# The combine stage's thirteen groups start with one node tile instead of ending with it

## The reference

```
x = x + ffn(layernorm(x))          # two experts per node, weighted
...
deg = count of each src;  dinv = (deg + 1) ** -0.5
msg = layernorm(x)[dst] * dinv[src] * dinv[dst]
agg = segment_sum(msg, src)        # self loops included
x = x + relu(agg @ W.T + b)
```

## Time and profile before

| what | value |
|---|---|
| runs, median (lowest to highest) | 1460.05 us (1455.34 to 1467.41) |
| the profiled execution's own time | 1453.73 us |
| its span | 1451.9 us |
| PE busy in the span | 1217.1 us (84%) |
| DVE, ACT, POOL busy | 855.9, 528.9, 396.1 us |
| mean granted TensorE clock | 0.926 of full speed |

### The profile page before, as it was taken

How to read it: one execution, slowest core, us unless ns; L and a number is a source line. 1 busy time by engine, 2 the same in 40 slices (tenths; PEclk the granted TensorE clock), 3 DMA queues, 4 the chain that set the end, 5 groups by cost and what they waited for, 6 DMA issues and landing times.

```text
span 1451.9 us, 31013 instructions
## 1 busy us (share of the span) xinstructions
PE 1217.1 (84%) x11970; PEld 1046.1 (72%) x11970; DVE 855.9 (59%) x1901; ACT 528.9 (36%) x1261; POOL 396.1 (27%) x309
## 2 busy tenths in 40 slices
PE   2366768899977999999999999948999999732995
PEld 1366667545657999999999999936888888622664
DVE  4899999814467787777777756667102233355211
ACT  0143536323244555555555565644101111210220
POOL 2044520000001453545454422223430111112213
PEclk8599989999987999999999999978999999955998
DMA  6455555200025666455677666579865555311101
GB/s 172 115 165 160 162 154 157 71 15 29 15 91 176 153 162 166 105 123 125 186 188 186 157 138 174 112 207 277 235 193 152 175 154 161 108 64 31 39 22 48
DMA packets 235005, 193.21 MB, mean 133 GB/s; under 512 B 155368, under 2 KB 189130, under 8 KB 234804
## 3 DMA queue, kind: packets, MB, share of 16 engines
q1 hardware_dynamic: 211006, 146.41, 37.7%
q0 software_dynamic: 15808, 37.72, 8.4%
q10 hardware_dynamic: 8038, 7.03, 1.6%
HBM read 131.17 MB, written 63.24 MB: 134 GB/s over the span
## 4 chain that ended last, share of the span: by engine, by line
PE 67%; DVE 14%; issue 7%; DMA 6%; POOL 3%; ACT 1%; SPq 1%; DVEq 0%; POOLq 0%; ACTq 0%
PE ps L1584 8%; PE ps L1593 8%; PE ps L1604 8%; PE ps L1556 8%; PE ps L1648 6%; PE ps L1649 6%; PE ps L1477 3%; PE ps L1491 3%; PE ps L1696 3%; DMA arena<-in_edge_attr_dram 3%; DVE arena L1030 3%; DVE arena L1019 2%; PE ps L1706 2%; DMA arena<-dp_scr,arena 2%; DVE arena L1034 2%
## 5 line engine op out<-in xcount | busy, mean ns | idle before, releaser
L823 ACT ACTIVATE arena<-ps 75x512 f16<-75x512 f32 x462 | 248.1, 591 | 161.8 <-PE ps L1556 161.8
L1648 PE MATMUL ps<-arena 126*128 126x256 f16 x1100 | 248.4, 277 | 31.2 <-DMA arena<-y_scr,yidx 29.9
L1649 PE MATMUL ps<-arena 126*128 126x256 f16 x1100 | 248.2, 277 | 0.0
L655 POOL DMA_INDIRECT y_scr<-arena,tok_out x64 | 148.4, 2318 | 283.9 <-DVE arena L1217 268.2
L1438 PE MATMUL ps<-arena 128*128 128x65 bf16 x976 | 122.0, 206 | 73.1 <-DVE arena L1034 72.9
L1438 PEld LDWEIGHTS ps<-arena 128*128 128x128 bf16 x976 | 109.4, 122 | 81.9 <-DVE arena L1034 62.6
L1174 DVE TENSOR_TENSOR arena<-iob,BB 128x1024 bf16<-128x1024 bf16 x231 | 158.1, 684 | 0.0
L1556 PE MATMUL ps<-arena 128*75 128x128 bf16 x1848 | 154.7, 221 | 3.5 <-DVE arena L1174 3.0
L1556 PEld LDWEIGHTS ps<-arena 128*75 128x75 bf16 x1848 | 134.5, 116 | 19.3 <-ACT arena L823 8.4
L1648 PEld LDWEIGHTS ps<-arena 126*128 126x128 f16 x1100 | 109.4, 99 | 47.6 <-issue 31.5
L1584 PE MATMUL ps<-arena 128*128 128x128 f32 x1024 | 131.2, 282 | 0.0
(11 more groups left out here) (314 smaller groups left out, 2099.1 us busy)
## 6 DMA issues: line engine op xcount, KB each, us to landing
a_scr<-arena SPq DMA_DIRECT2D x115, 300.0 KB, 4.6
arena<-in_edge_attr_dram SPq DMA_DIRECT2D x122, 256.0 KB, 2.9
arena<-in_L_ffn_w_dram SPq DMA_DIRECT2D x54, 512.0 KB, 4.3
arena<-a_scr SPq DMA_DIRECT2D x44, 315.0 KB
arena<-a_scr SPq DMA_DIRECT2D x44, 283.5 KB
arena<-a_scr SPq DMA_DIRECT2D x44, 189.0 KB
arena<-y_scr SPq DMA_DIRECT2D x24, 256.0 KB, 5.0
X<-in_x_dram ACTq DMA_DIRECT2D x1, 3072.0 KB
```

Of the source, the lines that this page charges most:

```text
L655: eng.indirect_dma_start(y2_d, bass.IndirectOffsetOnAxis(ap=tok_out[:, m:m + 1], axis=0), yb[:, i % 4, :], None, bounds_check=NT * 256 - 1 ...
L823: eng.activation(ev[0:75, m % NEV, 4 * (h % 4):4 * (h % 4) + 4, :], PS[ABANK[h % 3]][0:75, :].rearrange("p (s b) -> p s b", b=128), ACT.Id ...
L1648: eng.matmul(z, lhs, yv[0:KR, k, 0:256], start=(k == 0 and h == 0), stop=False)
L1649: ins = eng.matmul(z, lhs, yv[0:KR, k, 256:512], start=False, stop=(k == KT - 1 and (h == 1 or i == len(tiles) - 1)))
```

## The change

The groups are `[0], [1, 2], [3, 4], ... [23, 24]` in place of `[0, 1], [2, 3], ... [22, 23], [24]`: still 13. The wait of POOL before gather k follows the new bounds of the groups. All that loops over `COMB` (loads, adds, statistics, writes) follows too. What SP issues behind which group is as before.

```diff
-COMB = [list(range(a, min(a + 2, NT))) for a in range(0, NT, 2)]
+COMB = [[0]] + [[a, a + 1] for a in range(1, NT, 2)]
...
             for k in range(KT):
-                for g in range((y_rows(k) - 1) // 256 + 1):
+                for g in range(((y_rows(k) - 1) // 128 + 1) // 2 + 1):
                     e.wait_ge(st_y[g % NSY], 16 * (g // NSY + 1))
```

## The result

The changed kernel takes 1472.26 us in the median of 8 runs (1467.61 to 1476.23), the kernel before 1456.19 us in the median of 8 (1448.41 to 1467.41). The ratio is 1.0102, 95% interval 1.0069 to 1.0135: slower by about 15 us (16 by the medians). The forecast was 1475 us, 15 more than the 1460.05 that the kernel before had then.

What follows compares the result with a forecast made beforehand. Bound: a loop of waits in pass 0, writes of y standing on SP behind blocks that wait for steps. Four turns +8.5, half clock +4, step 7 +2.4: +14.9 on 1460.05 us, so 1475 us; range 1458 to 1486.

Steps and rivals of the forecast that it cites:

- step 0 earlier: Start of pass 0: one-tile first group sends write 0 and step 0 1.29 us earlier; gain does not reach step 2.
- step 7 later: Pass 0: step 3 waits for write 2, so step 7 starts at about 1004.5 us, 2.4 us late.
- from step 7 to step 23, more: Pass 0: four turns of 12.7 us, 50.8 where it was 42.28, +8.5 us; half clock in two, +4.
- from step 23 to the end of pass 0: Tail of pass 0: half clock behind step 23 adds up to 2.8 us.
- The end: Combine's last group: its pair adds 0.98 + 0.31 us of VectorE work, hidden by 9.9 us of cover; costs nothing.
- The turns: Pass 0 loop: odd step x's end, 1.6 us, write, L, then step x + 4; 12.7 us per four steps.
- handing over: SP, from a step's end to the write's issue: half of 2.49 us for one block plus handing over, 1.6 us.
- L: Path from a write's issue on SP to the start of the step waiting for it: 8.9 us taken, 9.53 last before.
- the relief: Less loaded DMA engines in pass 0 shorten L, to 8.1 us at light load; 8.9 taken.
- The clock: TensorE, idling 4.6 to 5.4 us per turn, restarts at half clock: 2.0 us per turn, 0 to 8; +4 taken.
- Nothing faster: Rival for pass 0: L under 7.2 us keeps the 1.3 us start gain; 1449 to 1459 us, chance 0.08.
- The transfers did not give way: Rival for pass 0: L mostly queueing, falling to 7.2 to 8 us; 0 to +4 us, chance 0.21.

Runs made afterwards that it cites:

- second profile: The changed kernel unaltered, run and profiled once more on another chip: ratio 1.0112; the profiled execution took 1464.94 us.
- The runs with lighter loads: Changed kernel, groups 4 to 12 loaded in 16 of 256 columns, for the second expert's rows (ratio 1.0041) or both experts' rows (1.0054).
- blocks one later: Changed kernel with SP issuing matrix blocks 2g + 3 and 2g + 4 behind write g, in place of 2g + 4 and 2g + 5: ratio 0.9969.
- the last experiment: Kernel before, old groups, with SP's blocks four later and y's writes issued from ScalarE's queue: ratio 0.9944.
- the lightest loads: Changed kernel with both experts' rows of groups 4 to 12 loaded in 16 of 256 columns, about 4.4 of 16 MB left out: ratio 1.0054.
- The wait alone: Kernel before, old groups, with only POOL's wait changed so gather 2g - 1 already waits for write g: ratio 1.0091.

## Why the prediction was right

Against the profiles, counted from the first add of Combine (the head start of step 0 is lost again before step 7 and is no term of the sum):

| step of the prediction | forecast | measured | second profile |
|---|---|---|---|
| step 0 earlier | 1.3 us | 1.8 us (12.70 to 10.88) | 1.8 |
| step 7 later | 2.4 | 3.4 (38.20 to 41.61) | 1.9 |
| from step 7 to step 23, more | 12.5 | 11.4 (42.28 to 53.66) | 6.6 (48.88) |
| from step 23 to the end of pass 0 | 0 to 2.8 | 0.0 (45.85 and 45.84) | 1.7 (47.51) |
| sum of the last three | 14.9 | 14.8 | 10.2 |

The direction and the loop behind it were right. The close match of the sum is partly luck: it holds for one execution of the changed kernel, and two wrong sizes made up for most of each other in it, as the turns show. The other signs came too: 26.88 us from write 8 to write 12, where I wrote 25 or more, and, with the 7.9 us of before the stage taken off, step 23 at 1059.1 and the end of pass 0 at 1105.0.

*The start.* The head start came and was lost at step 1, as written: step 1 waits 3.38 us and starts 18.6 us after the first add, where it was 16.9. It was somewhat worse than I took it, because step 5, which needs write 3, then waited 6.54 us; I had expected the first full wait at step 3. Write 3 stood behind block 9, which waited for the end of step 1 at 994.15, and its path to step 5 took 12.56 us (994.84 to 1007.40), nearly the 13.82 of group 2 before. In the second profile it took 9.85.

*The end.* The last pair cost nothing; its rows lay ready for 13.0 us (1044.1 to 1057.11).

*The turns.* A turn has the three terms of the prediction: one step, a handing over, L. Step 5 to step 9: 3.79 + 0.68 + 9.84 = 14.31 us. Step 9 to 13: 3.47 + 0.69 + 9.59 = 13.75. Step 13 to 17: 4.21 + 0.73 + 7.12 = 12.06. Step 15 to 19: 2.18 + 0.65 + 8.71 = 11.54. Step 19 to 23: 2.18 + 0.66 + 9.92 = 12.76. Step 19 hung on step 15 and not on 17, so there were two strands.

Two terms were mis-sized in opposite ways. I took 1.6 us for handing over, with half of the 2.49 us that the row of blocks 24 and 25 lasts. I had misread that row: block 25 needs the end of step 17, which came at 1031.96, and went out behind it, so the row holds one step (2.18 us) and one block (0.31):

```profile
1032.22 0.31 SPq L534 DMA_DIRECT2D arena<-a_scr  x1
1032.63 0.38 SPq L577 DMA_DIRECT2D y_scr<-arena  x1
```

Before, write 11 thus went out 0.67 us behind the end of step 17, and a turn was two steps, 0.67 and L, 14.56 us for six steps. Handing over is 0.7 us in both kernels. With it and my L of 8.9, four turns would have been 47.0 us and the forecast 3.8 us lower. And L was 9.6 to 9.9 in three of the five turns, 8.7 and 7.1 in the others. The 7.12 is not on the path to step 23; the four that are have a mean of 9.5 us where I took 8.9. So from step 7 to 23 the handing over was 3.7 us too high and L 2.4 us too low, which with the clock gives the 1.1 us between 12.5 and 11.4. The turns differ in the gather more than in the write: from step 5 to 9, 3.84 us passed until POOL issued the gather and 6.00 from there to the step, from step 13 to 17 it was 3.69 and 3.43. The runs with lighter loads show why the relief was overrated: L hardly falls with load.

*The clock.* Steps 5, 9 and 13 ran at or near half clock, behind 6.54, 3.81 and 3.56 us of idling, 1.3 to 2.0 us each above 2.18: 4.9 us together, of which 3.3 lie between steps 7 and 23; with step 14, which took 3.06 us behind step 13, the path there carries 4.2 us, where I took 4. The kernel before has 1.7 us of the same kind there, which I had overlooked: steps 10 and 11, behind 2.04 us of idling, took 2.97 and 3.06 us. But step 23, behind 3.40 us, ran at full clock. Behind step 0, five steps had waited for over 3.3 us; steps 1 (3.76 us long), 5, 9 and 13 were slow, step 23 was not. The Trainium skill's rule ("TensorE: Matmul & The Clock Gate", section "HAM oscillation — how this bites in real kernels"), by which each turn begins slow, thus held in four of five. How long TensorE idled does not settle it by itself: with blocks one later, step 13 took 3.30 us behind 2.45 us of idling, and in the last experiment step 4 took 2.28 us behind 3.77.

*The rivals.* Nothing faster came of it. The transfers did not give way: L was 7.12 us in one turn, 8.71 in another and 9.6 to 9.9 in three, and with the lightest loads, at two thirds of the load of before, still 8.5 to 9.1. But the rival was nearer than the prediction put it, since an L of 8.1 and not 7.2 us was enough for it. The Trainium skill's formula for one transfer ("DMA: Bandwidth & Descriptors", section "Anatomy of one DMA") would have made L 5.2 us; the section gives it for transfers that GpSimd issues, so it covers the gather and not SP's write. The only path near it is that of group 0 before, 5.46 us, and the first write of the changed kernel landed within 2.0 us.

*The mechanism itself* is shown from both sides. The wait alone brings 0.9% of loss, one block more ahead of the write brings 0.6% without the change, and one block less ahead of it, or the write on another queue, takes the loss away with the change in place. How the loss divides among the start, L and the clock rests on single profiles.

## What to carry to other kernels

When a group's bounds move, ask for each consumer which piece it needs first, and then what stands ahead of that piece's write on its queue; a shift by one can cost a step of cover in a loop that has none to spare. Idle times a fixed number of steps apart are the sign of such a loop, and its turn can be read off as step, handing over and transfer path. Don't put a transfer that others wait for behind one that waits for a free slot: issue the slot's refill later, or the transfer from another queue.

## What the hardware showed that I had not expected

From the write of group 5 on, the path from issuing a write of y to the start of the step that waits for it took 8.0 to 10.3 us in every turn but one (7.12) of the kernel before, the two profiles of the changed kernel and the one with the lightest loads, from 0.62 to 0.95 of the DMA engines' time, although the same two transfers took 5.46 us with little beside them. A write issued on ScalarE's queue with six more transfers of SP's queue issued ahead of it took 5.7 us to be seen, against 2.0 when SP had issued it ahead of those six: in this row, being on another queue did not let it pass them. In the last experiment, where twelve loads stood ahead of the write and the last of them had gone out 1.8 us before it, it took 2.9 us. And a row of two merged transfers on SP's queue can hold a wait: what reads as 2.49 us for two block loads was 0.31 us for one, the wait for a step, and 0.31 us for the other.
